# A two-layer graph network kernel: the sums of its second sweep and the scores of its first are issued in another way

## The reference

```python
x_l = (h @ W_l + b_l).reshape(n, H, F); x_r = (h @ W_r + b_r).reshape(n, H, F)
m = leaky_relu(x_l[src] + x_r[dst] + (ea @ W_e).reshape(-1, H, F), 0.2)
alpha = einsum('ehf,hf->eh', m, att)            # scores, then softmax over a node's edges
out = segment_sum(x_l[src] * alpha[..., None], dst, n).mean(axis=1) + bias
x = x + relu(batchnorm(out))
h = relu(layernorm(x))
x = x + mean over edges of h[src] @ w_l.T + h @ w_r.T + b
```

## Time and profile before

| | us |
|---|---|
| runs | 6172.38, 6160.61, 6160.41 (median 6160.61) |
| profiled execution, its own time | 6173.44 |
| its span | 6172.1 |
| mean granted TensorE clock | 0.79 |

### The profile page before, as it was taken

The page is one execution under the profiler, slowest core; times in us unless marked ns, Lnnn a source line. Parts: engine busy times, 40 slices in busy tenths (PEclk is TensorE's granted clock), DMA queues, the critical chain, the costliest instruction groups (busy, mean ns, idle before and its releaser), DMA issues. The chain is left out here.

```text
span 6172.1 us, 90375 instructions
## 1 busy us (share of the span) xinstructions
PE 4005.9 (65%) x16664; PEld 3028.2 (49%) x16665; DVE 3777.2 (61%) x19506; ACT 1160.5 (19%) x4355; POOL 3828.3 (62%) x3799
## 2 busy tenths in 40 slices
PE   2888888888888872888888886723333333333337
PEld 1666666666666661444444443613333333333336
DVE  6677777777777778888888889852222222222224
ACT  1111111111111111555555541200000000000001
POOL 2577777777777762544444451347777777777770
PEclk8999999999999996999999998655555555555555
DMA  7344444444444431333333331111111111111111
GB/s 105 104 132 130 130 130 131 131 130 130 131 132 129 131 107 43 94 90 90 92 92 93 90 85 30 35 41 26 26 26 26 26 26 26 26 26 26 26 26 24
DMA packets 633247, 478.13 MB, mean 77 GB/s; under 512 B 452024, under 2 KB 460344, under 8 KB 632812
## 3 DMA queue, kind: packets, MB, share of 16 engines
q1 hardware_dynamic: 468218, 258.72, 16.6%
q0 software_dynamic: 104800, 108.55, 9.3%
q10 hardware_dynamic: 60050, 109.22, 4.8%
HBM read 350.04 MB, written 126.05 MB: 77 GB/s over the span
## 5 line engine op out<-in xcount | busy, mean ns | idle before, releaser
L505 POOL DMA_INDIRECT ZR<-hD,mS x1664 | 1589.5, 955 | 612.6 <-issue 491.5
L1074 POOL DMA_INDIRECT BIG<-h2D,mS x1564 | 1481.3, 947 | 573.8 <-issue 472.4
L1095 PE MATMUL PS<-BIG,ZR 128*128 x3328 | 814.4, 428 | 1266.8 <-DMA BIG<-h2D,mS 1252.4
L572 DVE SCALAR_TENSOR_TENSOR PS<-PS,a 128x66 f32<-128x66 f32 x6656 | 1279.2, 258 | 523.2 <-PE PS L535 508.0
L1095 PEld LDWEIGHTS PS<-BIG,ZR 128*128 128x128 f32 x3328 | 740.0, 328 | 1341.4 <-DMA BIG<-h2D,mS 1326.1
L1109 DVE TENSOR_TENSOR BIG<-BIG,PS 128x64 f32 x1664 | 364.1, 219 | 1408.4 <-PE PS L1095 1366.8
L768 PE MATMUL PS<-rb,ZR 128*128 128x329 f32 x3328 | 1045.8, 458 | 217.8 <-DVE ZR L461 136.6
L534 PE MATMUL PS<-Wz,zo 128*128 128x264 f32 x3328 | 1025.3, 390 | 23.0 <-DVE PS L572 22.3
L535 PE MATMUL PS<-BIG,rb 128*128 x3328 | 1014.9, 387 | 0.0
L759 POOL TENSOR_TENSOR rb<-ZR,rb 128x768 f32<-128x768 f32 x416 | 615.1, 1479 | 633.6 <-ACT rb L749 606.3
L782 DVE TENSOR_TENSOR BIG<-BIG,PS 128x329 f32 x1664 | 823.9, 495 | 212.7 <-PE PS L768 147.1
(11 more groups left out here) (210 smaller groups left out, 2230.6 us busy)
## 6 DMA issues: line engine op xcount, KB each, us to landing
zD<-ZR ACTq DMA_DIRECT2D x416, 256.0 KB
ZR<-zD SPq DMA_DIRECT2D x416, 256.0 KB, 2.6
rb<-relD SPq DMA_DIRECT2D x105, 512.0 KB
ZR<-ea SPq DMA_DIRECT2D x1664, 32.0 KB
ZR<-hD,mS POOLq DMA_INDIRECT x1664, 2.4
BIG<-h2D,mS POOLq DMA_INDIRECT x1564, 2.4
AL<-hD SPq DMA_DIRECT2D x28, 224.0 KB, 2.8
lmS<-lmD SPq DMA_DIRECT2D x106, 32.0 KB, 2.2
```

Source lines behind the costliest of these rows:

```text
L505: Q.indirect_dma_start(zring[:, j % 32, 0, :], None, hD, bass.IndirectOffsetOnAxis(mS[:, j // 16, j % 16:j % 16 + 1], 0)).then_inc(hs[q], 16)
L572: k = V.scalar_tensor_tensor(m, m, 0.0, a84[:, h, :], ALU.max, ALU.mult, accum_out=alq[:, j // 16, 4 * (j % 16) + h:4 * (j % 16) + h + 1])
L1074: Q.indirect_dma_start(ACC[:, j % NB, j // NB * F:j // NB * F + F], None, h2D, bass.IndirectOffsetOnAxis(mS[:, (j // 16) % 4, j % 16:j % 1 ...
L1095: P.matmul(PS[:, j % 7, 0:F], oh[:, (j // 4) % 4, j % 4, :], rows, start=True, stop=True).then_inc(a3_rdy.s, 1)
```

## The change

**Second sweep.** The common loop is gone: each engine has its own loop of 64 slots (`load_quads`, `last_head`, `first_heads`, `sums2`, `adds2`), 26 passes. The rows have four slots of a quad (16 of a slot) instead of three; the tiles `Wr`, `zo` and `rb` are now parts of one tile `R`. DVE makes a one-hot for a single slot, 128 columns, by a tensor-scalar instruction that compares the row of numbers in PSUM with one number per partition (`onehot2`), twelve slots ahead of its use, one behind every add. Twelve of them stand before the loop. PE waits for `o2_rdy` per slot (by the counts in `TAKE2`) and, with `BANK2`, puts slot 63 of a pass into bank 3.

**First sweep.** The scores of two slots are made by one pair of instructions: `weighted` (max with 0 and product with `a8`, 2 x 264 columns in PSUM, without an accumulated sum), and a pair later `summed` (a reduction over 66 columns into eight scores). The products of a pair lie in two of six banks instead of one of four each, and PE waits for free banks once per pair. DVE's loop has 64 slots instead of 32.

```diff
-    gf, t_rdy, zo_rdy, oh_rdy, m_rdy, dv_done, go, fin = flows("p1_", 8)
+    gf, t_rdy, zo_rdy, oh_rdy, m_rdy, free1, wt_rdy, go, fin = flows("p1_", 9)
...
+    TAKE1 = [2, 1, 0] + [1] * 29
+    def scores_of(p):
+        return PS[:, 2 + 2 * (p % 3):4 + 2 * (p % 3), 0:MC]
...
-                for h in range(H):
-                    m = PS[:, 2 + j % 4, h * WC:(h + 1) * WC]
-                    k = V.scalar_tensor_tensor(m, m, 0.0, a84[:, h, :], ALU.max, ALU.mult,
-                                               accum_out=alq[:, j // 16, 4 * (j % 16) + h:4 * (j % 16) + h + 1])
+        def weighted(p):
+            m = scores_of(p)
+            return V.scalar_tensor_tensor(m, m, 0.0, bc(a8.unsqueeze(1), [128, 2, MC]), ALU.max, ALU.mult)
+        def summed(p):
+            return V.tensor_reduce(alq[...], scores_of(p).rearrange("p s (h c) -> p s h c", c=WC), AX.X, ALU.add)
...
+                weighted(p).then_inc(wt_rdy.s, 1)
+                if p % 2 == 1:
+                    onehots_turned(p // 2 + 2).then_inc(oh_rdy.s, 1)
...
+                if p > 0:
+                    wt_rdy.take(V)
+                    summed(p - 1).then_inc(free1.s, 1)
...
+    BANK2 = [j % 7 for j in range(63)] + [3]
+    TAKE2 = [0, 0, 0, 4, 0, 0, 0] + [1] * 56 + [4]
+    def onehot2(s):
+        return V.tensor_scalar(oh[:, (s // 4) % 4, s % 4, :], iota_ps, mR[:, (s // 16) % 4, s % 16:s % 16 + 1], None, ALU.is_equal)
...
-    with nc.Fori(0, NIT) as i:
...
+    def sums2():
+        o2_rdy.take(P, 3)
+        close(o2_rdy)
+        with P.Fori(0, NS // 64):
+            for j in range(64):
+                if j % 4 == 0:
+                    x_rdy.take(P)
+                    px_rdy.take(P)
+                if TAKE2[j]:
+                    o2_rdy.take(P, TAKE2[j])
+                P.matmul(PS[:, BANK2[j], 0:AC], oh[:, (j // 4) % 4, j % 4, :], rows2(j // 4)[:, j % 4, :],
+                         start=True, stop=True).then_inc(ag_rdy.s, 1)
+            close(x_rdy, px_rdy, o2_rdy)
+    def adds2():
+        with V.Fori(0, NS // 64) as i:
+            vt = Table(V, bT, i, "wb", NB - 1, 64)
+            for j in range(64):
+                a, s = ahead(V, BIG[:, ds(vt(j) * AC, AC)]), j + 12
                 ag_rdy.take(V)
-                V.sem_inc(rbf.s, 1)
-                V.sem_inc(hbf.s, 1)
+                if j % 4 == 3:
+                    V.sem_inc(rbf.s, 1)
+                    V.sem_inc(hbf.s, 1)
                 c2_acc.take(V)
+                V.tensor_tensor(a, a, PS[:, BANK2[j], 0:AC], ALU.add).then_inc(c2_acc.s, 1)
+                if s % 16 == 0:
+                    mr[(s // 16) % 4].take(V, 16)
+                onehot2(s % 64).then_inc(o2_rdy.s, 1)
+                if j % 16 == 15:
+                    V.sem_inc(mrf.s, 1)
+            close(ag_rdy, c2_acc, *mr)
```

More of the change, by code:

```diff
@@ L720, in build, with rows2 @@
     v(V.tensor_copy(iota_ps, iota))
+    BANK2 = [j % 7 for j in range(63)] + [3]
+    TAKE2 = [0, 0, 0, 4, 0, 0, 0] + [1] * 56 + [4]
+    def rows2(q):
+        return R[:, 4 * (q % 4):4 * (q % 4) + 4, :]
+    def onehot2(s):
+        return V.tensor_scalar(oh[:, (s // 4) % 4, s % 4, :], iota_ps, mR[:, (s // 16) % 4, s % 16:s % 16 + 1], None, ALU.is_equal)
     mr[0].take(V, 16)
-    onehots(0).then_inc(o2_rdy.s, 1)
+    for s in range(12):
+        k = onehot2(s)
+    k.then_inc(o2_rdy.s, 6)
@@ new lines, in load_quads @@
+    def load_quads():
+        with S.Fori(0, NS // 64) as i:
+            for q in range(16):
+                half, k = q // 4, q % 4
+                if k == 1:
+                    mrf.take(S)
+                    load_rel(ds(i * 4 + half + 2, 1), (half + 2) % 4)
+                    load_maxima((i * 4 + half + 2) * 64, (half + 2) % 4)
+                hbf.take(S)
+                S.dma_start(hb[:, k, :, :, :].rearrange("p s t f -> p (s t f)"),
+                            zD[ds(i * 16 + q, 1), :, :].rearrange("a p c -> (a p) c")).then_inc(hq[k].s, 16)
+            close(mrf, hbf)
@@ new lines, in last_head @@
+    def last_head():
+        with A.Fori(0, NS // 64) as i:
+            for q in range(16):
+                k = q % 4
+                alq4 = ahead(A, AL[:, ds(i * 256 + 16 * q, 16)].rearrange("p (s h) -> p s h", h=4))
+                rbf.take(A)
+                r = rows2(q)
+                A.copy(r[:, :, 256:260], alq4).then_inc(hx.s, 1)
+                if k == 0:
+                    ml[(q // 4) % 4].take(A, 16)
+                A.copy(r[:, :, 260:264], lmS[:, (q // 4) % 4, 16 * k:16 * k + 16].rearrange("p (s h) -> p s h", h=4)
+                       ).then_inc(lm_st.s, 1)
+                hq[k].take(A, 16)
+                A.copy(r[:, :, 265:329], hb[:, k, :, 1, :]).then_inc(hz.s, 1)
+                lm_st.take(A)
+                for n in range(4):
+                    ins = A.activation(r[:, n, 192:256], hb[:, k, n, 0, :], ACT.Copy, scale=r[:, n, 259:260])
+                ins.then_inc(x_rdy.s, 1)
+            close(rbf, lm_st, *hq, *ml)
@@ new lines, in first_heads @@
+    def first_heads():
+        with Q.Fori(0, NS // 64):
+            for q in range(16):
+                hx.take(Q)
+                hz.take(Q)
+                r = rows2(q)
+                Q.tensor_tensor(r[:, :, 0:192].rearrange("p s (h f) -> p s h f", f=F),
+                                bc(hb[:, q % 4, :, 0, :].unsqueeze(2), [128, 4, 3, F]),
+                                bc(r[:, :, 256:259].unsqueeze(3), [128, 4, 3, F]), ALU.mult).then_inc(px_rdy.s, 1)
+            close(hx, hz)
+    def sums2():
[3 more added lines that the diff above has]
+            for j in range(64):
+                if j % 4 == 0:
+                    x_rdy.take(P)
[5 more added lines that the diff above has]
+            close(x_rdy, px_rdy, o2_rdy)
@@ L782, in build @@
-            V.tensor_tensor(a, a, PS[:, j % 7, 0:AC], ALU.add).then_inc(c2_acc.s, 1)
-            if j == G - 1 or j % 4 == 0 and j != G - 4:
-                q = j // 4 + 1
-                if q % 4 == 0:
-                    mr[(q // 4) % 4].take(V, 16)
-                onehots(q).then_inc(o2_rdy.s, 1)
-            if j % 16 == 15:
-                V.sem_inc(mrf.s, 1)
-        close(*hq, *ml, *mr, mrf, hz, o2_rdy, hx, x_rdy, px_rdy, ag_rdy, rbf, hbf, c2_acc, lm_st)
+                V.tensor_tensor(a, a, PS[:, BANK2[j], 0:AC], ALU.add).then_inc(c2_acc.s, 1)
```

121 lines of the change are left out of this document (40 added, 81 removed).

## The result

The changed kernel takes 6257.97 us (median of 4 runs, 6249.42 to 6272.91), the kernel before 6161.24 on the same chip: a ratio of 1.0155, 95% interval 1.0133 to 1.0178. The forecast was 6128, its range ended at 6178. The change is slower by 97 us, and the forecast was wrong in sign.

A forecast was written before the change was run, and what follows sets the result against it. POOL's gather issue bounds the first and third sweeps, DVE the second. There 128 slots take 93.6 instead of 96.3 us: 35 us less, 2.5 back at the last edge, so 6160.6 - 33, about 6128 us; range 6030 to 6178.

The forecast's parts named there:

- the edge: Second sweep, DVE between passes: without the engines' meeting, 2.7 us from add to add, twice per 128 slots.
- The one-hot: Second sweep, DVE: 128 columns out of PSUM with a number per partition take 338 ns.
- add and one-hot: Second sweep, DVE: one add with its one-hot takes 0.66 us a slot, 79.2 us for 120 slots.
- the table step: Second sweep, DVE: add to add across the table load, once per 16 slots, takes 1.5 instead of 1.54 us.
- PE keeping up: Second sweep: PE needs at most 0.58 us a slot against DVE's 0.66, so it holds nothing up.
- The number for each partition: Second sweep, DVE's one-hot: reading one number per partition costs a tensor-scalar instruction some 58 ns.
- The floor of a slot: Second sweep, DVE: the add's wait for the add before keeps a slot from falling below about 0.60 to 0.64 us.
- D: Rival, second sweep's edge: the jump itself is long and comes 26 times, 65 us lost, 6193 us; chance 0.08.
- A: Rival, second sweep: one-hot as cheap as from SBUF, 0.196 us, slot 0.60 us, 6035 us; chance 0.15.
- B: Rival, second sweep: next add waits for the one-hot's end, slot 0.74 us, 125 us lost, 6253 us; chance 0.08.
- C: Rival, first sweep: gathers meet turned one-hots more often, 34 us eat the gain, 6162 us; chance 0.14.
- The DRAIN you can't avoid: Skill section weighed for second-sweep DVE: no start before the pipe empties, so 0.84 us a slot, 281 us more.

The follow-up runs named there:

- e4: Kernel before with its common loop over all engines cut to 64 slots, plus the changed kernel's first sweep and four row slots; 0.9938 of the kernel before.
- f1: Changed kernel with its DVE second-sweep pass moved by 41 instructions executed once ahead of the loop; 0.9896 of the kernel before.
- e6: Changed kernel with DVE's passes cut to 32 slots and single one-hots made by TENSOR_TENSOR; 0.9788 of the kernel before.
- e8: Kernel before with the changed kernel's first sweep alone; 0.9952 of the kernel before.
- f2: Changed kernel with one-hots made in pairs, 32 idle DVE increments a pass, moved by 9 instructions; single run, 159 transfers, edge 6.05 us.
- f4: e5 moved by 45 instructions executed once ahead of the loop; single run, 35 transfers, jump 0.27 us, sweep 1210.3 us.
- e5: Changed kernel with one-hots made in pairs and 64 idle DVE increments a pass; 1.0045 of the kernel before.
- e9: Changed kernel with single one-hots made by TENSOR_TENSOR instead of TENSOR_SCALAR, passes of 64 slots; 1.0025 of the kernel before.
- f3: e9 moved by 41 instructions executed once ahead of the loop; 0.9787 of the kernel before.

## Why the prediction was wrong

**The step that failed** is the edge: "the edge of a loop of one engine is seen in the third sweep: 1.11 us ... it is 2.7 us from add to add". It measured 6.18 us. The row was read rightly, but the third sweep's pass has 246 rows of DVE and isn't read again (jump 0.3 us), and the second sweep's was, already in the kernel before. I put the 4.33 and 4.50 us <-issue of the earlier trace rows down to the meeting of engines. "Issue" says that the profile shows no releaser; the jump of 3.2 us and ten instruction transfers in a pass, five of them DVE's, were in the trace, and the prediction read neither. e4, which keeps the meeting and ends the reading, has an edge of 2.65 us. The term was then doubled: leaving the common loop went with passes of half the length, so 13 jumps became 26.

**A term that was missing** is what stands behind a long edge. PE starts no product between 2806.06 and 2810.40 (3.63 us idle), returns at 1.2 GHz, and DVE catches up with it at the fourth addition. The third to the seventh interval behind an edge take 4.43 us in the changed kernel and 3.38 in f1, 1.05 us a pass.

The two together: edge (6.18 - 2.50) x 25 = 92 us, slow start 1.05 x 25 = 26, sum 118; the sweeps of the changed kernel and f1 differ by 117.5.

**What was right.** The one-hot 345 ns (338), add and one-hot 0.665 us (0.66), the table step 1.40 (1.5), PE keeping up, the rows never waited for, the first sweep's instructions 717 and 698 ns (700) with the gathers still setting its pace on the chip of the result. With the edge as in f1, the sweep is 1214.4 us against 1246.2 before, 32 us less; the forecast had 33. So the sum was right for the kernel that isn't read again, its small errors nearly cancelling. The number for each partition was priced at 58 ns, and e6 shows 61 (345 - 284). The floor of a slot was put at 0.60 to 0.64 us; e6 has 0.604.

**The rivals.** D said that the jump itself is long and comes 26 times. It named the right term, with 0.08 of the chance, but not the cause: the jump is long only where the pass is read again, and takes 0.3 us in f1. Its price was too small, since it took 5.2 us for the edge of before, which runs from the last one-hot; from add to add it is 5.53. With what was measured, 26 x (6.18 + 1.05 - 5.2) = 53 us more brings its 6193 to 6246, near the 6258 measured. A (a one-hot of 0.196 us) is excluded for this instruction by 345 ns; its 0.60 us a slot is what TENSOR_TENSOR reaches. B (0.74 us a slot) is excluded by 0.665. C (gathers that meet turned one-hots) by 957 ns for 955. The rule of the Trainium skill weighed there, "The DRAIN you can't avoid", would have had 0.84 us a slot, and 0.665 disagrees once more. The section itself excepts an instruction that isn't held, which starts earlier; the prediction left that out.

**What a rule would have told.** The re-reading is shown by the transfers and the jumps of the table. The Trainium skill, "Runtime: NRT & Kernel Launch", section "Instruction fetch mechanics", states that a taken branch to a target outside the window held forces a fetch before execution goes on. The runs agree with that. It gives blocks of 16 KiB, 256 instructions, two of them held. In one point the runs differ: DVE's transfers are of 8192 B, at a spacing of 128 rows. In the other they don't decide. By blocks of 256 rows with borders at 182, 438, 694 and 950, two held, every second-sweep loop of the table comes out as measured too: the passes that are read again touch three such blocks (the kernel before's 570 to 1050 and e8's 395 to 875 among them), the others one or two.

**What stays open.** The borders are known to within some three rows, and their place is fitted, though f1, f2 and f4 were foretold from it. That the place decides is shown by the moved kernels. How much is held is not: three blocks of 128 rows and two of 256 fit all traces. A pass that touches four of the first kind and only two of the second, rows 445 to 925 say, would tell, and none was run. That the kernel before's pass is at 570 and not at 442 rests on the count of transfers ahead of it.

## What to carry to other kernels

Before a loop is split or its edge is priced, look at its jump and at the transfers of kind instruction. If they come in every pass, the pass is too long for its place. Here that made the edge 2.7 to 3.8 us longer (e5 against f4, e9 against f3), besides up to 1.9 us behind it. Keep each engine's pass under some 256 rows (it then touches at most three blocks of 128, or two of 256, wherever it lies), or look where it lies: a few rows once ahead of the loop can be worth more than the change itself. A wait put down to "issue" is a question and not an answer.
